# Second stage of a two-layer convolution: three tap products and a partial sum added by TensorE, moments on ScalarE

## Chip, cores and metric

The kernel runs on one core of a Trainium2 chip. The metric is the device time of one execution in microseconds (us); the time of the kernel before is the median of three runs.

## What is computed

The input x is (16, 512, 64, 64) in fp32. Two layers of the form x + conv(group_norm(x)) follow each other. The first is a 4x4 blur of every channel. The second, cut to what matters:

```python
x = x + _L0_conv_ref(_gn(x), L0_conv_kernel)
x = x + _L1_conv_ref(_gn(x), ...)

def _L1_conv_ref(x, w_v, w1, gn_gamma, gn_beta, w2, b2):
    t = relu(group_norm(d4_1x1(x, w1), gn_gamma, gn_beta, cmid))      # 256 channels
    wgt = einsum('oi,bighw->boghw', w2, t) + b2                       # 9 tap weights of each group and pixel
    ...                                                               # taps turned for each of 8 orientations
    pats = unfold_patches(d4_1x1(x, w_v), 3)                          # 3x3 patches of 512 channels
    return (wv * pats).sum(axis=4)                                    # sum of 9 products
```

So each output is a residual plus nine products of a tap weight with a shifted value.

## The kernel before

`stage_a` (the first quarter of the time) does the blur and is not touched. It leaves its result x1 in HBM. `stage_b` does the second layer, image by image.

**The pieces of an image.** On TensorE an image has eight chunks of 512 pixels a band: `forward` (L716, 4 PSUM banks a chunk), `block_v` (4 banks) and `block_t` (2 banks) by `block_of` (L726), and `inverse` (L742, 2 banks). They make the value maps `xm` and the map `t`. They are made during the period of the image before, at the steps that FORWARD_AT, BLOCK_V_AT, BLOCK_T_AT and INVERSE_AT name (L78 to L81). `values` (L749) turns `xm` into `val`, three granules ahead. `tap_weights` (L765) makes the nine tap weights of a quarter of the image (a unit) in PSUM banks 0 to 4.

**The granule.** An image has 16 granules of 4 channel maps (4 units by 4). For each, with 1024 elements a partition, VectorE (`granule`, L1127) makes six products of taps 3 to 8 (`pooled`, L1088) into the ring `prod_p` and, in two halves of 512 columns (`opening`, L1100), three products of taps 0 to 2 that it adds itself, with the residual, through PSUM bank 7 and into `acc`. GpSimd (L1018 to L1029) adds the six products of the ring, one after another, to `acc`. Each of its additions waits for its own last one by `p_added`. SP then stores `acc`, and had loaded the residual into it.

**The ring of banks.** All results that ScalarE fetches from PSUM (`forward`, `block`, `inverse`, `values`) go through the two banks 5 and 6. TensorE's `take` (L696) waits until ScalarE has emptied the bank two before, and ScalarE takes them in the same order.

**What sets the order.** Each engine has one queue written out by hand: a period of 16 steps, step n holding what belongs to granule n. TensorE's period is L825 to L844, ScalarE's L973 to L997, VectorE's L1157. At the end of a period `lead` (L790, L939) makes the first values and taps of the next image.

**The moments of t.** VectorE takes statistics of t (`t_stats`, `t_aggregate`), TensorE averages over partitions (`means`, `variances`), VectorE does the small arithmetic between (`t_spreads`, `t_add_eps`, `t_affine`, L1054 to L1074), GpSimd the power (`t_rstd_of`, L1012), ScalarE then `relu` (L932). The bias of a tap is added in PSUM by ScalarE (`tap_bias`, L925).

Of the kernel before, what the change touches and what calls it, by code (L numbers as in the profile page):

```python
# [24 lines left out]
ALU = mybir.AluOpType  # L25
# [42 lines left out]
D_TAPS, P_TAPS = (0, 1, 2), (3, 4, 5, 6, 7, 8)  # L68
NP = len(P_TAPS)
P_RING = 4  # L70
P_LATE = (4, 5)
HALF = 512
WV_BANKS = 5
ACC_RING = 4
# [7 lines left out]
LOAD_AT = {1: 1, 2: 2, 3: 3, 5: 4, 7: 5, 8: 6, 9: 7}  # L82
LOAD_NEXT_AT = 10
EDGES_AT = 13
RSTD_AT = (13, 5)
EDGES = 2
SETUP = 4
# [367 lines left out]
def stage_b(nc, ctx, sem, ps, x1, basis, wsrc, signs, w2t, w2mask, b2t, gamma, beta, mean_b, out, x1_scale, x1_bias):  # L455
    def sb(name, shape, dtype=F32):
# [7 lines left out]
    t_last = sb("t_last", [P, MT, BANDS * UPX])  # L464
# [12 lines left out]
    power = sb("power_b", [P, MT])  # L477
    six = sb("six_t", [P, MT, 2 * UNITS, 6])
# [12 lines left out]
    first_of = base[:, 3 * P:3 * P + 32]  # L491
    w_term = prod_p[:, 0, 0:2 * 4 * OQ * 16].rearrange("p (b c o) -> p b c o", b=2, c=4)
# [6 lines left out]
    sp_apart, act_apart, dve_apart = (sem(f"b_{e}_apart") for e in ("sp", "act", "dve"))  # L499
    setup = sem("b_setup")  # L500
# [11 lines left out]
    own = sem("own")  # L512
# [12 lines left out]
    OWN = 12  # L525
    EARLY, LATE = (0, 1, 2), (3, 4)
# [3 lines left out]
    def order_of_period(more):  # L530
        for n in range(N_GRAN):
            if n + AHEAD < N_GRAN:
                yield ("values", n + AHEAD), V_BANKS[n + AHEAD]
            if more:
                if n in BLOCK_V_AT:
                    yield ("block_v", BLOCK_V_AT[n]), QM
                for c in BLOCK_T_AT.get(n, ()):
                    yield ("block_t", c), MT
                if n in FORWARD_AT:
                    yield ("forward", FORWARD_AT[n]), IRR  # L540
                for c in INVERSE_AT.get(n, ()):
                    yield ("inverse", c), MT

    def order_at_first():
        yield ("forward", 0), IRR
        for c in range(CHUNKS):
# [4 lines left out]
            yield ("inverse", c), MT  # L551

# [13 lines left out]
    def taps_of(tap):  # L566
        return ps[:, tap // 2, tap % 2 * UPX:(tap % 2 + 1) * UPX]
# [16 lines left out]

    def t_end(i, u):

        return chunk_end(i, "inverse", 2 * u + 1)
# [5 lines left out]
    def bank_done(i, n, b):  # L593

        if b == 0:
            return own, i * (OWN * N_GRAN) + OWN * n + 8
        return p_done(i, n, P_TAPS.index(banks[b][-1]))

    def granule_done(i, n):

        return p_done(i, n, NP - 1)
# [26 lines left out]
    def _(sp):  # L628
# [11 lines left out]
        def load_resid(i, n):  # L640
# [29 lines left out]
        def period(i, more=True, ahead=True, begin=False):  # L670
            for n in range(N_GRAN):
# [19 lines left out]
    def _(pe):  # L691
# [11 lines left out]
        def affine():  # L703

            for kt in range(KT):
                q = slice(32 * kt, 32 * kt + 32)
                nc.tensor.matmul(ps[q, D_BANK, 0:B], first_of,
                                 x1_scale[:].rearrange("p (b k) -> p k b", k=KT)[:, kt, :], start=True, stop=True,
                                 skip_group_check=True)
                for r in range(IRR):  # L710
                    mm = nc.tensor.matmul(ps[q, D_BANK, (1 + r) * B:(2 + r) * B], forward_m[:, r, :],
# [53 lines left out]
        def tap_weights(i, u, which):  # L765
            pe.wait_ge(t_ready, i * (MT * UNITS) + MT * (u + 1))
            for b in which:
                if not first(i, u):
                    pe.wait_ge(*bank_done(i, GRANS * u - 1, b))
                for tap in banks[b]:  # L770
# [8 lines left out]

        def means(i):  # L780
            pe.wait_ge(t_local, i + 1)
            if not first(i):
                pe.wait_ge(*p_done(i, -3, NP - 1))
            nc.tensor.matmul(ps[:, STAT_BANK, MEAN0:MEAN0 + MT], blk[:], mv[:, :, 0], start=True, stop=True).then_inc(t_mean, 1)

        def variances(i):
            pe.wait_ge(t_spread, i + 1)
            nc.tensor.matmul(ps[:, STAT_BANK, VAR0:VAR0 + MT], blk[:], spread[:], start=True, stop=True)                .then_inc(t_var, 1)

        def lead(i):  # L790
# [34 lines left out]
        def period(i, more=True):  # L825
# [449 lines left out]
```

## Time and profile before

| | us |
|---|---|
| median of 3 runs | 5196.51 |
| fastest of them | 5195.63 |
| slowest of them | 7707.95 |
| the profiled execution's own time | 5195.25 |
| its span in the trace | 5193.5 |

The profiled execution has one core, so its span is that of all views. An engine is called busy while an instruction of it runs. Durations of neighbouring instructions of an engine overlap a little, so the pace of an engine is read from start to start. TensorE's clock is given as a share of 2.4 GHz; 0.50 is 1.2 GHz.

### The profile page before, as it was taken

The page shows a single profiled execution, that of the slowest core. Times are in us where ns is not written, and L with a number is a line of the kernel's source. Part 1 is how long each engine was busy: PE and PEld are TensorE (multiplying, and loading weights), DVE is VectorE, ACT ScalarE, POOL GpSimd, SP SyncE. Part 2 cuts the span into 40 slices and gives each one's busy share as a digit, 9 for nine tenths or more (in the row PEclk, how much of TensorE's full clock was granted, in tenths as well). Part 3 has the DMA queues.
Part 4 walks back from the last instruction along what each step waited for, and adds up shares of the span by engine and source line. Part 5 has one row for each costly group of instructions (what it writes and reads, how often), then busy time and mean ns, then how long its engine had stood idle before and what let it go on. Part 6 is the DMA issues. An engine that isn't in the chain of part 4 may idle for free.

```text
span 5193.5 us, 113938 instructions
## 1 busy us (share of the span) xinstructions
PE 3796.5 (73%) x36988; PEld 1315.4 (25%) x36988; DVE 4670.5 (90%) x8017; ACT 2854.0 (55%) x4642; POOL 4507.4 (87%) x2208
## 2 busy tenths in 40 slices
PE   8999999978766767676858685767676766767642
PEld 3333333322222222222222221222222222222220
DVE  6777777736999999999999999999999999999998
ACT  7999999956444535354545454444454444535421
POOL 5888888835999999999999999999999999999999
PEclk9999999989888888898889798989898988888866
DMA  7999999943333333232324242323232333333221
GB/s 235 257 257 257 257 256 256 247 107 100 105 102 102 99 106 107 92 121 83 119 83 130 83 127 85 120 91 115 91 110 91 110 103 102 99 106 107 82 74 57
DMA packets 872814, 679.40 MB, mean 131 GB/s; under 512 B 560080, under 2 KB 822736, under 8 KB 855888
## 3 DMA queue, kind: packets, MB, share of 16 engines
q1 hardware_dynamic: 872272, 672.72, 44.2%
q8 instruction: 273, 4.47, 0.4%
q14 instruction: 269, 2.20, 0.1%
HBM read 404.15 MB, written 268.44 MB: 130 GB/s over the span
## 4 chain that ended last, share of the span: by engine, by line
POOL 51%; DVE 13%; issue 9%; PE 4%; POOLq 1%; ACT 1%; DMA 0%; DVEq 0%; SPq 0%; ACTq 0%
POOL acc L1027 51%; DVE prod_p L1078 3%; DVE ps L1122 2%; DVE ps L1119 2%; DVE ps L1078 1%; DVE six_t L1043 1%; DVE acc L1125 1%; DVE prod_d L1078 1%; PE ps L722 1%; PE ps L732 1%; PE ps L773 1%; DVE dev_t L1059 1%; POOLq L1024 1%; DMA xr<-x 0%; POOLq L1026 0%
## 5 line engine op out<-in xcount | busy, mean ns | idle before, releaser
L1027 POOL TENSOR_TENSOR acc<-acc,prod_p 128x1024 f32<-128x1024 f32 x1536 | 3645.0, 2373 | 267.6 <-DVE acc L1125 50.4
L1078 DVE TENSOR_TENSOR prod_p<-ps,val 128x1024 f32<-128x1024 f32 x1536 | 1852.5, 1210 | 111.2 <-POOL acc L1027 110.7
L290 PE MATMUL ps<-xn,band 64*64 64x512 f32 x8192 | 949.2, 599 | 22.1 <-issue 13.7
L773 PE MATMUL ps<-t,w 128*32 128x256 f32 x9216 | 614.0, 425 | 435.7 <-ACT t L936 225.5
L760 PE MATMUL ps<-xm,base 128*32 128x256 f32 (+1 forms) x8192 | 636.2, 445 | 166.4 <-ACT val L923 73.7
L732 PE MATMUL ps<-xh,wh 128*32 128x512 f32 x6144 | 706.8, 600 | 49.6 <-ACT val L923 33.7
L1078 DVE TENSOR_TENSOR prod_d<-ps,val 128x512 f32<-128x512 f32 x1024 | 693.1, 677 | 25.7 <-ACT ps L929 24.0
L722 PE MATMUL ps<-xr,base 128*32 128x512 f32 x4096 | 547.1, 659 | 213.3 <-ACT val L923 124.1
L923 ACT ACTIVATE val<-ps 128x512 f32<-128x512 f32 (+1 forms) x640 | 339.8, 555 | 619.5 <-DVE prod_p L1078 418.0
L322 POOL TENSOR_TENSOR x_out<-x_out,x_in 128x512 f32<-128x512 f32 x512 | 636.2, 1275 | 0.0
L250 ACT ACTIVATE x_out<-ps 64x512 f32<-64x512 f32 x1024 | 606.1, 592 | 52.1 <-PE ps L290 31.8
L929 ACT ACTIVATE ps<-ps,b 128x256 f32<-128x256 f32 x576 | 235.2, 444 | 508.6 <-PE ps L773 506.8
L871 ACT ACTIVATE xh<-ps,xh_affine 128x512 f32<-128x512 f32 x512 | 395.1, 777 | 195.5 <-PE ps L722 180.0
L773 PEld LDWEIGHTS ps<-t,w 128*32 128x32 f32 x9216 | 309.2, 121 | 756.4 <-DVE ps L1119 219.6
L290 PEld LDWEIGHTS ps<-xn,band 64*64 64x64 f32 x8192 | 325.3, 132 | 434.0 <-issue 430.0
L337 POOL TENSOR_TENSOR rstd<-var_eps,power 128x8 f32 (+2 forms) x133 | 212.9, 1601 | 238.1 <-DVE var_eps L384 238.1
L879 ACT ACTIVATE xm<-ps 128x512 f32<-128x512 f32 x512 | 306.0, 598 | 190.4 <-PE ps L732 190.4
L760 PEld LDWEIGHTS ps<-xm,base 128*32 128x32 f32 x8192 | 251.2, 115 | 563.8 <-issue 186.4
L237 ACT ACTIVATE xn<-x_in,norm_b,rstd 128x512 f32<-128x512 f32 x512 | 389.5, 809 | 6.6
L916 ACT ACTIVATE val<-val 128x512 f32<-128x512 f32 x192 | 120.5, 628 | 436.7 <-DVE prod_p L1078 436.6
L1078 DVE TENSOR_TENSOR ps<-ps,val 128x512 f32<-128x512 f32 x512 | 351.2, 686 | 0.0
L1119 DVE TENSOR_TENSOR ps<-ps,acc 128x512 f32<-128x512 f32 x512 | 351.2, 686 | 0.0
(73 smaller groups left out, 3180.1 us busy)
## 6 DMA issues: line engine op xcount, KB each, us to landing
x_in<-x SPq DMA_DIRECT2D x128, 1024.0 KB, 7.4
x<-x_out SPq DMA_DIRECT2D x256, 512.0 KB, 5.2
xr<-x SPq DMA_DIRECT2D x512, 256.0 KB, 3.5
acc<-x SPq DMA_DIRECT2D x1024, 128.0 KB, 2.9
out<-acc SPq DMA_DIRECT2D x256, 512.0 KB, 2.7
prod_p<-wsrc SPq DMA_DIRECT2D x1, 384.0 KB, 4.6
w<-w2t SPq DMA_DIRECT2D x1, 288.0 KB, 4.6
shift_m<-shifts SPq DMA_DIRECT2D x1, 256.0 KB, 5.5
```

Source lines behind the costliest of these rows:

```text
L237: nc.scalar.activation(group(xn[:, r, :], XP, W, 2, g), group(x_in[:, k % X_RING, :], W, W, 0, g), ACT.Identity, bias=norm_b[:, k % 2, g:g ...
L250: nc.scalar.activation(group(x_out[H2 * t:H2 * t + H2, r, :], W, W, 0, 2 * two + x).rearrange("p m h w -> p m (h w)"), ps[at:at + H2, 2 * ...
L290: mm = nc.tensor.matmul(ps[to:to + H2, 2 * two + t, :], band[rows, v, rows], group(xn[rows, k % N_RING, :], XP, W, v, 2 * two + x), start= ...
L322: nc.gpsimd.tensor_tensor(out, out, group(x_in[:, k % X_RING, :], W, W, 0, g) .rearrange("p m h w -> p m (h w)"), ALU.add).then_inc(x_adde ...
L722: mm = nc.tensor.matmul(ps[32 * kt:32 * kt + 32, b, :], forward_m[:, r, :], xr[:, kt, :], start=True, stop=True, skip_group_check=True)
L732: mm = nc.tensor.matmul(ps[32 * r:32 * r + 32, b, :], wh[:, r, o, :], xh[:, c % 2, r, :], start=True, stop=True, skip_group_check=True)
L760: mm = nc.tensor.matmul(ps[32 * q:32 * q + 32, b, at:at + ROWS[u] * W], inverse_v[:, m + x, :], xm[:, q4, r0:r0 + ROWS[u] * W], start=True ...
L773: mm = nc.tensor.matmul(taps_of(tap)[32 * q:32 * q + 32, :], w2[:, kt, tap * 32:(tap + 1) * 32], t[:, kt, u, q * UPX:(q + 1) * UPX], start ...
L871: nc.scalar.activation(xh[:, c % 2, r, :], ps[:, b, :], ACT.Identity, bias=xh_affine[:, 1 + r, bass.ds(i, 1)], scale=xh_affine[:, 0, bass. ...
L1027: nc.gpsimd.tensor_tensor(acc[:, r, :], acc[:, r, :], prod_p[:, k % P_RING, :], ALU.add).then_inc(p_added, 1)
L1078: return nc.vector.tensor_tensor(dst.rearrange("p (m r w) -> p m r w", m=count, w=W), taps_of(tap).rearrange("p (m r w) -> p m r w", m=1, ...
L1119: nc.vector.tensor_tensor(ps[:, D_BANK, :], ps[:, D_BANK, :], acc[:, r, half], ALU.add).then_inc(own, 1)
```

## The change

In the text below sum 0 and sum 1 are the two calls of the new `sums` for a granule, and final 0 and final 1 those of the new `final`.

- GpSimd's partial sum is of taps 0 to 5. VectorE writes tap 0's product straight into a new tile `sum_p` (ring of 2), and GpSimd adds the products of taps 1 to 5 to it.
- VectorE writes the products of taps 6 to 8 in full width into `prod_d`.
- TensorE adds the four terms (three of `prod_d`, one of `sum_p`) by multiplying them with the identity in tiles of 64x64, in two halves of a granule. Each half is 4 terms by 4 matmuls of 256 columns.
- VectorE adds that sum and the residual into `acc`, 512 columns at a time (`final`). `acc` has a ring of 2 in place of 4. The order of the parts in `acc` is new, so the residual comes in 8 DMAs and not 4, and the host unpacks the output another way.
- The banks of the taps and of the ring are other ones (ring in banks 6 and 7; sums in the second halves of banks 4 and 5).
- The small arithmetic on the moments of t goes from VectorE to ScalarE (ten small activations and the two reads of PSUM). The tile `t_last` is gone.
- The steps at which the pieces are made are moved, and `lead` is dissolved into steps 15 and 0.

The diff, cut to its core:

```diff
-D_TAPS, P_TAPS = (0, 1, 2), (3, 4, 5, 6, 7, 8)
+P_TAPS, D_TAPS = (0, 1, 2, 3, 4, 5), (6, 7, 8)
+NA = NP - 1
-ACC_RING = 4
+S_RING = 2
+ACC_RING = 2
+TAP_BANKS = {0: (0, 1), 1: (2, 3), 4: (5,), 2: (4, 6), 3: (7, 8)}
-FORWARD_AT = {0: 0, 1: 1, 2: 2, 4: 3, 6: 4, 7: 5, 8: 6, 9: 7}
-BLOCK_V_AT = {1: 0, 2: 1, 4: 2, 5: 3, 8: 4, 9: 5, 12: 6, 13: 7}
-BLOCK_T_AT = {1: (0,), 2: (1,), 4: (2,), 5: (3,), 8: (4,), 9: (5,), 10: (6, 7)}
-INVERSE_AT = {1: (0,), 2: (1,), 4: (2,), 5: (3,), 8: (4,), 9: (5,), 11: (6, 7)}
+FORWARD_AT = {0: 0, 1: 1, 2: 2, 5: 3, 6: 4, 7: 5, 9: 6, 10: 7}
+INVERSE_AT = {2: (0,), 3: (1,), 5: (2,), 6: (3,), 9: (4,), 10: (5,), 13: (6, 7)}
+BLOCK_V_AT = {1: 0, 2: 1, 4: 2, 5: 3, 8: 4, 9: 5, 13: 6, 14: 7}
+BLOCK_T_AT = {1: (0,), 2: (1,), 4: (2,), 5: (3,), 8: (4,), 9: (5,), 12: (6, 7)}
+STATS_AT = {4: 0, 7: 1, 11: 2, 13: 3}
+MOMENTS_AT, EDGES_AT = 14, 14
+RSTD_AT = (14, 2)
...
 # SP, step n
-                if more or n + 2 < N_GRAN:
-                    load_resid(i, n + 2)
                 if not (begin and n == 0):
                     store(i, n - 1)
+                    if more or n + 1 < N_GRAN:
+                        load_resid(i, n + 1)
...
 # TensorE
+        def sums(i, n, half):
+            if half == 0:
+                wait_apart(pe, pe_apart, *d_done(i, n, ND - 1))
+                wait_apart(pe, pe_apart, p_added, i * (NA * N_GRAN) + NA * (n + 1))
+                if n % GRANS == GRANS - 1 and n < N_GRAN - 1:
+                    wait_apart(pe, pe_apart, tap_ready, tap_count(i, (n + 1) // GRANS, 4))
+            if not first(i, n + half):
+                wait_apart(pe, pe_apart, *(final_done(i, n, 0) if half else final_done(i, n - 1, 1)))
+            terms = [prod_d[:, j, :] for j in range(ND)] + [sum_p[:, n % S_RING, :]]
+            for j, term in enumerate(terms):
+                for t in range(2):
+                    for x in range(2):
+                        rows, to, at = slice(H2 * t, H2 * t + H2), H2 * (t ^ x), (2 * half + x) * UPX
+                        mm = nc.tensor.matmul(ps[to:to + H2, SUM_BANKS[1 - t], UPX:], same[rows, :],
+                                              term[rows, at:at + UPX], start=(j == 0), stop=(j == len(terms) - 1),
+                                              skip_group_check=True)
+            mm.then_inc(summed, 1)
...
+            for n in range(N_GRAN):
+                u = n // GRANS
+                if n % GRANS == 0:
+                    tap_weights(i, u, TAP_ORDER[2:4])
+                if more and n == MOMENTS_AT:
+                    means(i + 1)
+                if more and n in FORWARD_AT:
+                    forward(i + 1, FORWARD_AT[n])
+                if more:
+                    for c in INVERSE_AT.get(n, ()):
+                        inverse(i + 1, c)
+                if not (begin and n == 0):
+                    sums(i, n - 1, 0)
+                if more and n == MOMENTS_AT:
+                    variances(i + 1)
+                if n % GRANS == 0:
+                    tap_weights(i, u, TAP_ORDER[4:])
                 if n + AHEAD < N_GRAN:
                     values(n + AHEAD)
+                if more and n == N_GRAN - 1:
+                    pe.wait_ge(xm_edges, EDGES * (i + 2))
+                    values(0)
+                if not (begin and n == 0):
+                    sums(i, n - 1, 1)
                 if more:
                     if n in BLOCK_V_AT:
                         block_v(i + 1, BLOCK_V_AT[n])
                     for c in BLOCK_T_AT.get(n, ()):
                         block_t(i + 1, c)
...
                 if n % GRANS == GRANS - 1 and n < N_GRAN - 1:
-                    tap_weights(i, n // GRANS + 1, EARLY)
-            if more:
-                lead(i + 1)
+                    tap_weights(i, u + 1, TAP_ORDER[:2])
+                if more and n == N_GRAN - 1:
+                    values(1)
+                    tap_weights(i + 1, 0, TAP_ORDER[:1])
+                    values(2)
+                    tap_weights(i + 1, 0, TAP_ORDER[1:2])
...
 # GpSimd
-                for j in range(NP):
-                    nc.gpsimd.tensor_tensor(acc[:, r, :], acc[:, r, :], prod_p[:, k % P_RING, :], ALU.add).then_inc(p_added, 1)
+                for j in range(1, NP):
+                    nc.gpsimd.tensor_tensor(total, total, prod_p[:, k % P_RING, :], ALU.add).then_inc(p_added, 1)
...
 # VectorE, granule n
+            if not begin:
+                for j in range(ND):
+                    direct(i, n - 1, j)
...
+            pooled(i, n, 0)
+            pooled(i, n, 1)
             pooled(i, n, 2)
+            if not begin:
+                final(i, n - 1, 0)
             pooled(i, n, 3)
+            pooled(i, n, 4)
+            if not begin:
+                final(i, n - 1, 1)
+            pooled(i, n, 5)
```

ScalarE follows TensorE's order. Its step 15 is `t_affine`, `relu` of unit 0, `keep_values` 0, `keep_values` 1, bias of bank 0, `relu` 1, `keep_values` 2, bias of bank 1, `relu` 2.

## Rows read from the trace of the kernel before

**Rows 1.** The page: busy time of each engine, and the two costliest groups.

```profile
PE 3796.5 (73%) x36988; PEld 1315.4 (25%) x36988; DVE 4670.5 (90%) x8017; ACT 2854.0 (55%) x4642; POOL 4507.4 (87%) x2208
...
L1027 POOL TENSOR_TENSOR acc<-acc,prod_p 128x1024 f32<-128x1024 f32 x1536 | 3645.0, 2373 | 267.6 <-DVE acc L1125 50.4
L1078 DVE TENSOR_TENSOR prod_p<-ps,val 128x1024 f32<-128x1024 f32 x1536 | 1852.5, 1210 | 111.2 <-POOL acc L1027 110.7
```

**Rows 2.** Timeline of GpSimd, one period: start, duration (us), line, operation, idle before.

```profile
2189.91 0.71 POOL L1014 TENSOR_TENSOR rstd_t<-var_eps_t,power_b 128x2 f32<-128x2 f32 x1 [3.70 <-DVE var_eps_t L1065]
2190.59 14.82 POOL L1027 TENSOR_TENSOR acc<-acc,prod_p 128x1024 f32<-128x1024 f32 x6
2207.35 181.35 POOL L1027 TENSOR_TENSOR acc<-acc,prod_p 128x1024 f32<-128x1024 f32 x72 [1.94 <-DVE acc L1125]
...
2437.69 0.71 POOL L1014 TENSOR_TENSOR rstd_t<-var_eps_t,power_b 128x2 f32<-128x2 f32 x1 [3.71 <-DVE var_eps_t L1065]
```

**Rows 3.** Timeline of VectorE: the statistics of a unit; inside a granule.

```profile
1203.43 2.47 DVE L1043 BATCH_NORM_STATS2 six_t<-t_last 128x6 f32<-128x512 f32 x4 [17.32 <-ACT t_last L894]
...
1982.84 0.69 DVE L1119 TENSOR_TENSOR ps<-ps,acc 128x512 f32<-128x512 f32 x1
1983.43 1.21 DVE L1078 TENSOR_TENSOR prod_p<-ps,val 128x1024 f32<-128x1024 f32 x1
1984.56 0.69 DVE L1122 TENSOR_TENSOR ps<-ps,prod_d 128x512 f32<-128x512 f32 x1
```

**Rows 4.** Timeline of TensorE in its dense stretches of the second stage.

```profile
1995.31 1.93 PE L760 MATMUL ps<-xm,base 128*32 128x256 f32 x32
1997.29 5.49 PE L732 MATMUL ps<-xh,wh 128*32 128x512 f32 x48
2002.64 1.92 PE L722 MATMUL ps<-xr,base 128*32 128x512 f32 x16
2004.72 1.93 PE L722 MATMUL ps<-xr,base 128*32 128x512 f32 x16 [0.15 <-ACT xh L871]
2006.78 1.99 PE L747 MATMUL ps<-t,base 128*128 128x512 f32 x4
2008.70 1.93 PE L760 MATMUL ps<-xm,base 128*32 128x256 f32 x32
...
2139.01 5.39 PE L773 MATMUL ps<-t,w 128*32 128x256 f32 x96
```

**Rows 5.** Timeline of TensorE in the first stage, tiles of 64x64 and of 128x128 in turn.

```profile
602.75 3.70 PE L290 MATMUL ps<-xn,band 64*64 64x512 f32 x32
606.37 0.39 PE L271 MATMUL ps<-mv,ones 128*128 128x8 f32 x2
606.93 3.70 PE L290 MATMUL ps<-xn,band 64*64 64x512 f32 x32 [0.17 <-issue]
```

**Rows 6.** Instructions of ScalarE in one period by line and shape.

```profile
L929 ACT ACTIVATE ps<-ps,b 128x256 f32<-128x256 f32 x36 | 14.7, 443 | 33.0 <-PE ps L773 32.8
...
L936 ACT ACTIVATE t<-t,t_bias,t_scale 128x1024 f32<-128x1024 f32 x6 | 7.0, 1232 | 0.0
```

**Rows 7.** Timeline of TensorE: a `forward` after an idle stretch.

```profile
2072.76 6.60 PE L722 MATMUL ps<-xr,base 128*32 128x512 f32 x32 [6.48 <-ACT val L923]
```

**Rows 8.** Window of that stretch; last three columns: granted clock, DMA share, GB/s.

```profile
2072.00:2076.00 4.00, 3.24 (x16) 0.74 (x20) 4.00 (x7) 1.87 (x3) 3.71 (x3) 0.50 0.21 45
```

**Rows 9.** Timeline of GpSimd, last period: its second granule and its last.

```profile
4949.99 14.86 POOL L1027 TENSOR_TENSOR acc<-acc,prod_p 128x1024 f32<-128x1024 f32 x6 [0.17 <-DVE prod_p L1078]
...
5175.51 14.77 POOL L1027 TENSOR_TENSOR acc<-acc,prod_p 128x1024 f32<-128x1024 f32 x6 [0.17 <-POOL acc L1027]
```

**Rows 10.** Timeline of SP's queue: the four DMAs of a residual.

```profile
1984.28 1.85 SPq L650 DMA_DIRECT2D acc<-x  x4
```

**Rows 11.** The page, DMA issues: KB each, us from issue to landing.

```profile
acc<-x SPq DMA_DIRECT2D x1024, 128.0 KB, 2.9
out<-acc SPq DMA_DIRECT2D x256, 512.0 KB, 2.7
```

More of the change, by code:

```diff
@@ L566, in taps_of, with bank_of, tap_count @@
     def taps_of(tap):
-        return ps[:, tap // 2, tap % 2 * UPX:(tap % 2 + 1) * UPX]
+        bank = next(b for b in TAP_ORDER if tap in TAP_BANKS[b])
+        h = TAP_BANKS[bank].index(tap)
+        return ps[:, bank, h * UPX:(h + 1) * UPX]
+    def bank_of(tap):
+        return next(b for b in TAP_ORDER if tap in TAP_BANKS[b])
+    def tap_count(i, u, bank):
+        return i * (UNITS * len(TAP_ORDER)) + len(TAP_ORDER) * u + TAP_ORDER.index(bank) + 1
     def period_base(i):
@@ L591, in p_done, with d_done, bank_done, sums_done @@
         return p_ready, i * (NP * N_GRAN) + NP * n + j + 1
[L593 to L597, printed above, removed]
+    def d_done(i, n, j):
+        return d_ready, i * (ND * N_GRAN) + ND * n + j + 1
+    def bank_done(i, n, bank):
+        tap = TAP_BANKS[bank][-1]
+        return p_done(i, n, P_TAPS.index(tap)) if tap in P_TAPS else d_done(i, n, D_TAPS.index(tap))
+    def sums_done(i, n, half):
+        return summed, i * (2 * N_GRAN) + 2 * n + half + 1
+    def final_done(i, n, half):
+        return finished, i * (2 * N_GRAN) + 2 * n + half + 1
     def granule_done(i, n):
-        return p_done(i, n, NP - 1)
+        return d_done(i, n, ND - 1)
     def halo_count(i, n):
@@ L769, in tap_weights @@
                     pe.wait_ge(*bank_done(i, GRANS * u - 1, b))
-                for tap in banks[b]:
+                for tap in TAP_BANKS[b]:
                     for kt in range(MT):
@@ L849, in _ @@
         period(B - 1, more=False)
+        for half in range(2):
+            sums(B - 1, N_GRAN - 1, half)
     @block.scalar
@@ L882, in keep_block_t @@
         def keep_block_t(i, c):
-            if c >= CHUNKS - 2 and not first(i):
-                act.wait_ge(t_ready, i * (MT * UNITS))
             for m in range(MT):
@@ L962, in _ @@
             keep_inverse(0, c)
+        act.wait_ge(const_in, 16 * 6)
+        keep_means(0)
+        keep_variances(0)
         edges(0)
+        t_affine(0)
+        relu(0, 0)
         keep_values(0, 0)
-        relu(0, 0)
-        act.wait_ge(const_in, 16 * 6)
-        tap_bias(0, 0, EARLY + LATE)
+        tap_bias(0, 0, TAP_ORDER[:2])
         keep_values(0, 1)
@@ L994, in period @@
                 if n % GRANS == GRANS - 1 and n < N_GRAN - 1:
-                    tap_bias(i, u + 1, EARLY)
-            if more:
-                lead(i + 1)
+                    tap_bias(i, u + 1, TAP_ORDER[:2])
+                if more and n == N_GRAN - 1:
+                    keep_values(i + 1, 1)
+                    tap_bias(i + 1, 0, TAP_ORDER[:1])
+                    relu(i + 1, 1)
+                    keep_values(i + 1, 2)
+                    tap_bias(i + 1, 0, TAP_ORDER[1:2])
+                    relu(i + 1, 2)
         period(0)
@@ L1127, in granule, with final @@
+        def final(i, n, half):
+            r = n % ACC_RING
+            dve.wait_ge(*sums_done(i, n, half))
+            if half == 0:
+                dve.wait_ge(resid_in[r], i * (128 * N_GRAN // ACC_RING) + 128 * (n // ACC_RING + 1))
+            part = acc[:, r, half * HALF:(half + 1) * HALF].rearrange("p (s n) -> p s n", s=2)
+            total = ps[:, SUM_BANKS[0]:SUM_BANKS[1] + 1, UPX:]
+            nc.vector.tensor_tensor(part, total, part, ALU.add).then_inc(finished, 1)
         def granule(i, n, more, begin=False):
@@ L1194, in _ @@
         period(B - 1, more=False)
-        for j in P_LATE:
-            pooled(B - 1, N_GRAN - 1, j)
+        for j in range(ND):
+            direct(B - 1, N_GRAN - 1, j)
+        for half in range(2):
+            final(B - 1, N_GRAN - 1, half)
 PERMS = ((0, 1, 2, 3, 4, 5, 6, 7), (3, 0, 1, 2, 5, 6, 7, 4), (2, 3, 0, 1, 6, 7, 4, 5), (1, 2, 3, 0, 7, 4, 5, 6),
```

305 lines of the change are left out of this document (135 added, 170 removed).

## The prediction

> **What bounds the kernel now.** I read the page first. GpSimd and VectorE are the busy engines, TensorE is at 73% of the span, and the costliest group is GpSimd's additions into `acc`, of 2.37 us each [rows 1]. Then GpSimd's timeline, which shows how tight that chain is: 72 additions take 181.35 us without a pause, so 2.52 us from start to start, 0.15 of it the wait for its own last result. The power of the moments comes once an image and gives the period: 2437.69 - 2189.91 = 247.8 us [rows 2]. 96 additions by 2.52 are 241.9; the rest is the pause around the moments (3.70 waiting for the variance, 0.71 the power, 1.94 waiting for VectorE). So the second stage, three quarters of the time, runs at GpSimd's pace. The first stage isn't touched.
>
> **What the change does to each engine, by granule.** All paces are from start to start.
>
> GpSimd: 5 additions and not 6, of the same shape: 5 x 2.52 = 12.6 us, from 15.1 [rows 2].
>
> VectorE: a product of 1024 columns takes 1.13 us (1983.43 to 1984.56), an operation of 512 columns 0.60 [rows 3]. Nine products and two finals: 9 x 1.13 + 2 x 0.60 = 11.4 us. At steps 4, 7, 11 and 13 the statistics add 2.4 [rows 3]. The small arithmetic on the moments leaves it.
>
> TensorE: this is where the work goes. At full clock, in dense stretches: a chunk of `block` (6 banks) 5.35 us (1997.29 to 2002.64), so 3.57 for `block_v` and 1.78 for `block_t`; `forward` 4.14 (I use 4.1); `inverse` 1.92; `values` 1.95 for 32 instructions of 256 columns; 96 instructions for six taps 5.39, so 0.89 for a tap and 1.8 for a bank of two [rows 4]. For the four banks of 384 columns at an image's start I take 2.7, three quarters of 4 x 0.89. A half sum has 16 matmuls in tiles of 64x64. The first stage runs the same form with 512 columns, 32 instructions (two for each fp32 matmul, so 16 matmuls) in 602.75 to 606.37 = 3.62 us [rows 5]; with 256 columns that is 1.81. I take 1.8 for a half, 3.6 for a granule, 57.6 for an image. The image's other pieces: 8 `forward` 32.8, 8 `block` 42.8, 8 `inverse` 15.4, `values` 4 x 2.7 + 12 x 1.95 = 34.2, 36 taps 32. Together 215 us: below the old period, and above GpSimd's 16 x 12.6 = 202. TensorE becomes the fullest engine.
>
> But its work is lumpy, and the new order leaves little room to even that out. VectorE waits for sum 0 of granule n-1 at final 0, between its third and fourth product of granule n. GpSimd has by then only two products to add. So every step that is long on TensorE stops all three. I write P(n) for TensorE's time from the end of sum 0 of granule n-1 to that of granule n (`values` and bank 3 at unit starts, sum 1, `block`, taps, then `forward` and `inverse` of step n+1, sum 0): P(0) 12.2, P(1) 16.9, P(2) 12.8, P(3) 11.8, P(4) 18.7, P(5) 16.9, P(6) 9.7, P(7) 11.8, P(8) 18.7, P(9) 16.9, P(10) 5.6, P(11) 11.8, P(12) 14.8, P(13) 7.2, P(14) 7.2, P(15) 22.1. For instance P(4) = bank 3 1.8 + `values` 1.95 + sum 1 1.8 + `block` 5.35 + `forward` 4.1 + `inverse` 1.92 + sum 0 1.8.
>
> Two other limits stand against P(n). VectorE's cycle: 11.4, with statistics 13.8. And GpSimd's loop: from final 0 to the second product of the next granule is 10.3, five additions are 12.6, sum 0 with its wakeups 2.0: 24.9 for two granules, 12.5 for one. Going through the steps with all three, the distance from final 0 to final 0 is, for n from 1 to 15 and then 0: 16.9, 12.8, 12.1, 18.7, 16.9, 11.4, 13.8, 18.4, 16.9, 11.4, 13.8, 14.5, 14.4, 14.3, 22.1, 12.2. The sum is 240.6 us, against 247.8. So of the 40 us that GpSimd is spared in an image, TensorE's long steps take back all but 7.
>
> Now what a queue in order adds to that.
> - Step 15: ScalarE is behind. `relu` costs 1.2 an instruction, two for a unit, and a bias 0.44 [rows 6]. `relu` 1 stands ahead of `keep_values` 2, so `values(2)` finds its third bank not empty for about 2.6 us; `relu` 2 does the same to `forward(0)` for about 0.7. I take 3.3. `t_affine` and `relu` 0 come in the slack of step 14 and cost nothing; if the power of step 14 were late by more than 3 us, they would push into step 15 one for one.
> - Each half sum has waits of its own in TensorE's queue and changes the shape of the tiles and back. The first stage pays 606.93 - 606.37 = 0.56 for two such changes, two small instructions and a wait, 0.17 of it idle [rows 5]. So a half sum pays between 0 and 0.56; it counts only in the ten steps that TensorE sets. I take 0.15, near to that idle, as the small instructions are part of the 0.56: 20 x 0.15 = 3.0 (bounds 0 and 11.2).
> - The clock. After 6.48 us idle, a `forward` of four banks took 6.60 and not 4.1, at a clock of 0.50 [rows 7, 8]. The new order leaves TensorE idle for some 6 us in steps 10, 13 and 14. At 10 and 13 a slow sum is hidden, as GpSimd's next additions don't wait for it; ahead of step 15 it isn't: I take 2.0 (bounds 0 and 6).
>
> That makes 240.6 + 3.3 + 3.0 + 2.0 = 248.9 us a period, 1.1 more than now. Fifteen periods prepare a next image: +16.
>
> The last period has only `values`, taps and sums on TensorE, and goes at GpSimd's pace. Now it is 15.05 a granule, 241 for 16 [rows 9]; then 16 x 12.6 = 202, and behind it the last two sums and finals, 6. That saves 33, and less if the sums run at half clock (the loop is then 26.7 for two granules): I take 30, bounds 20 and 35.
>
> Costs that I set at nothing. The residual: the ring of 2 makes its load wait for the last store, but from final 1 it is 2.7 (landing of the store) + 8 issues at 0.46 + 2.9 = 9.3 us, and final 0 of that granule comes about 20 us later [rows 10, 11]. The loads of x1 stand in front of them in SP's queue, each waiting for a `forward` that TensorE has done by then. ScalarE's ten small activations replace VectorE's in step 14, in slack; without it they would cost some 2 us. The pause of 6.3 us around the moments [rows 2] goes.
>
> The sum: 5195 (own time of the profiled execution, 1.3 under the median) + 16 - 30 = 5181; to the median 5182.
>
> **Rivals.**
> - *The queue is smoother than I put it* (faster). Without relu stall, changes of tiles and cold clock: 240.6 a period, 15 x (-7.2) - 35 = -143, so 5053. For it: TensorE is at full clock wherever it is dense, and each P(n) is made of measured paces. If a long step could besides borrow from a short one by 1 us each, it would be 4900. Against: TensorE's queue is in order and the waits of sum 0 stand in it.
> - *Changing the tile shape costs TensorE at each half sum* (slower). It is one mechanism: 64x64 for the sums, 128x32 for all around. The row's ceiling is 0.56 a half sum [rows 5]; with it in the ten steps, 240.6 + 3.3 + 11.2 + 2.0 = 257.1, 15 x 9.3 - 25 = +115, so 5310. It turns the sign from 0.20 a half sum on, and costs over 2% from some 0.5. For it: nothing before switches in the second stage between 128x32 and 64x64. Against: in the first stage two switches, two instructions and a wait fit in that 0.56. The Trainium skill, TensorEngine Tiling, section Key Properties, says that changing the tiling mode (not just the tile) drains TensorE. By that rule 64 changes an image each empty the engine, and this rival is the one to expect; the first stage's row agrees that something is paid, and leaves open how much is the drain.
> - *The half sums are slower than half of a 512-column blur* (slower). A weight load of 64 columns for each 256 columns of moving data may not be hidden; the bound is the full 3.6 us of the 512-column row. At 2.6 a half: +16 a period, 5420. Against: taps with 256 columns run at 0.056 an instruction, half of 512's 0.111 [rows 4].
> - That the change doesn't do what it says I leave out: the operations are all there in the diff.
>
> **Chances.** Forecast (within 2%, about what a measurement tells from no change) 0.48. Smoother 0.27, faster by over 2% all of it. Tile changes 0.17 and slow half sums 0.08, slower by over 2%. The likeliest case's own range is 5100 to 5280. The range over the cases: 5030, where the smooth schedule and a little borrowing end, to 5330.
>
> **What would show it.** GpSimd's additions in groups of five at 2.52, with pauses of 4 to 7 us at steps 4, 5, 8, 9 and 15 released by VectorE, whose own idle time is at final 0 and released by the sums. TensorE over 80% busy in the second stage, at a clock above 0.9. Half sums of 1.8 to 1.95. Period 245 to 253 from power to power. The last period some 205. Wrong if VectorE's idle is at `tap_ready` or the residual, if half sums take over 2.2, or if the period is below 240.

## The result and the profile after

The changed kernel takes 5360.7 us (median of 4 runs, 5356.7 to 5362.7) against 5196.8. The ratio is 1.0315, with an interval of 1.0295 to 1.0335: 3% slower. I had forecast 5182, no change, with a range up to 5330, and it lies above that. The ratio and all comparisons below leave out two single runs that lie far off the rest, one of the kernel before (7708 us) and one of experiment 7 (10720 us).

The page of the kernel after: busy times, TensorE's clock in 40 slices, the chain that ended last, and the groups that answer to [rows 1].

```profile
PE 4678.5 (87%) x53372; PEld 1923.4 (36%) x53372; DVE 3950.6 (74%) x6113; ACT 2911.8 (54%) x4802; POOL 3903.2 (73%) x1953
...
PEclk9999999989999999999989898999999999999987
...
PE 52%; DVE 9%; issue 7%; POOL 6%; ACT 5%; DVEq 0%; POOLq 0%; ACTq 0%; DMA 0%; SPq 0%
...
L1128 POOL TENSOR_TENSOR sum_p<-sum_p,prod_p 128x1024 f32<-128x1024 f32 x1280 | 3041.4, 2376 | 1087.9 <-DVE prod_p L1154 1009.9
...
L833 PE MATMUL ps<-prod_d,base 64*64 64x256 f32 x12288 | 867.7, 417 | 426.4 <-POOL sum_p L1128 256.7
L1190 DVE TENSOR_TENSOR acc<-ps,acc 128x512 f32<-128x512 f32 x512 | 353.6, 691 | 923.9 <-PE ps L833 922.7
```

GpSimd got its 600 us less, and stands idle for 1088 us before its additions, waiting for products of VectorE. VectorE stands idle for 923 us before the finals (L1190), waiting for the sums of TensorE (L833). TensorE, 73% busy before, is now 87% busy and carries half of the chain. So the bound moved to TensorE, as I had put it; what that costs is where the forecast failed.

Timeline of GpSimd of the kernel after: the power of the moments in two neighbouring images, which answers to [rows 2].

```profile
2225.78 0.71 POOL L1116 TENSOR_TENSOR rstd_t<-var_eps_t,power_b 128x2 f32<-128x2 f32 x1
...
2485.22 0.72 POOL L1116 TENSOR_TENSOR rstd_t<-var_eps_t,power_b 128x2 f32<-128x2 f32 x1
```

This period is 259.4 us. I had forecast 248.9. The mean of 14 periods is 260.0, from 1450.17 to 5089.57; read the same way, the kernel before has 248.0. The 14 periods make 168 us of the 167 that the span grew. The first period adds 6.9, the start of the stage saves 2.5, and what stands behind the last power saves 4.8, where I expected 30 from the last period. So of the 179 us between forecast and result some 155 come from the periods and 25 from the end.

**Where in the period.** I go through it by the ends of sum 0 on TensorE, as the prediction did: step n is the time from the end of sum 0 of granule n-1 to that of granule n, so its last piece stands in step n+1 of the queue. The distances of one period in us:

| step | 1 | 2 | 3 | 4 | 5 | 6 | 7 | 8 | 9 | 10 | 11 | 12 | 13 | 14 | 15 | 0 |
|---|---|---|---|---|---|---|---|---|---|---|---|---|---|---|---|---|
| predicted | 16.9 | 12.8 | 12.1 | 18.7 | 16.9 | 11.4 | 13.8 | 18.4 | 16.9 | 11.4 | 13.8 | 14.5 | 14.4 | 14.3 | 22.1 | 12.2 |
| measured | 17.1 | 13.8 | 12.6 | 18.8 | 17.1 | 11.7 | 14.7 | 18.8 | 17.0 | 13.5 | 14.9 | 14.7 | 15.6 | 14.5 | 30.5 | 14.4 |

The period they make up is 259.4 us against 240.6. Of the 18.8 between them I had put 8.3 on top. Step 15 has 8.4 of it, steps 0 and 10 4.3, steps 7, 11 and 13 3.2, step 2 1.0.

Timeline of TensorE of the kernel after. First step 4, from the end of one sum 0 (2325.63) to that of the next (2344.40); then step 10; then step 15.

```profile
2325.63 1.93 PE L812 MATMUL ps<-t,w 128*32 128x256 f32 x32
2327.38 1.91 PE L799 MATMUL ps<-xm,base 128*32 128x256 f32 x32
2329.22 1.53 PE L833 MATMUL ps<-prod_d,base 64*64 64x256 f32 x24
2330.57 0.61 PE L833 MATMUL ps<-sum_p,base 64*64 64x256 f32 x8
2331.11 5.49 PE L771 MATMUL ps<-xh,wh 128*32 128x512 f32 x48
2336.46 1.93 PE L761 MATMUL ps<-xr,base 128*32 128x512 f32 x16
...
2340.60 1.98 PE L786 MATMUL ps<-t,base 128*128 128x512 f32 x4
2342.52 1.53 PE L833 MATMUL ps<-prod_d,base 64*64 64x256 f32 x24
2343.86 0.61 PE L833 MATMUL ps<-sum_p,base 64*64 64x256 f32 x8
2344.40 1.93 PE L799 MATMUL ps<-xm,base 128*32 128x256 f32 x32
...
2433.46 2.84 PE L833 MATMUL ps<-prod_d,base 64*64 64x256 f32 x24 [6.01 <-POOL sum_p L1128]
2436.04 1.10 PE L833 MATMUL ps<-sum_p,base 64*64 64x256 f32 x8
2437.08 2.55 PE L799 MATMUL ps<-xm,base 128*32 128x256 f32 x32
...
2506.12 1.47 PE L799 MATMUL ps<-xm,base 128*32 128x384 f32 x16
2509.90 2.69 PE L799 MATMUL ps<-xm,base 128*32 128x384 f32 x16 [2.31 <-ACT val L1018]
2512.35 2.47 PE L812 MATMUL ps<-t,w 128*32 128x256 f32 x32
2517.31 4.25 PE L812 MATMUL ps<-t,w 128*32 128x256 f32 x48 [2.49 <-DVE prod_p L1154]
```

Step 4 is dense, and each piece has the price of [rows 4]. A half sum takes 1.89 (2329.22 to 2331.11) where I had 1.8 + 0.15, so the changes of tile shape cost no more than I had put. In step 10 TensorE is idle for 6.01 us and the half sum then takes 3.6 (2433.46 to 2437.08). Step 15 shows three losses: 2.3 for ScalarE's `relu` 1, a gap of 2.5 that I had not seen coming, and slow matmuls behind each gap (rows of 2.69 for 1.47, 2.47 for 1.91, 4.25 for some 2.7; from start to start some 3 us in all).

Windows of the half sum in step 10 and behind the two gaps of step 15; the last three columns are clock, DMA share, GB/s.

```profile
2433.00:2437.00 4.00, 3.54 (x32) 1.97 (x32) 3.12 (x3) 0.39 (x1) 1.85 (x1) 0.50 0.37 108
2510.00:2512.00 2.00, 2.00 (x16) 0.71 (x20) 0.88 (x1) 0.72 (x2) 0.95 (x1) 0.51 0.25 72
2518.00:2520.00 2.00, 2.00 (x24) 0.95 (x20) 0.00 (x0) 0.45 (x1) 1.57 (x1) 0.50 0.01 4
```

The clock is 0.50 in the first and the third and 0.51 in the second, so 1.2 GHz.

### The profile page after: what moved, and what is told of

Same layout as the page of the kernel before. It is cut to its first block, busy times and chain, and to the rows that moved or that the text cites. A ratio compares the mean times of both kernels' runs of the same rounds, so it can differ in the third digit from the quotient of the medians.

```text
span 5360.9 us, 147175 instructions
## 1 busy us (share of the span) xinstructions
PE 4678.5 (87%) x53372; PEld 1923.4 (36%) x53372; DVE 3950.6 (74%) x6113; ACT 2911.8 (54%) x4802; POOL 3903.2 (73%) x1953
## 4 chain that ended last, share of the span: by engine, by line
PE 52%; DVE 9%; issue 7%; POOL 6%; ACT 5%; DVEq 0%; POOLq 0%; ACTq 0%; DMA 0%; SPq 0%
PE ps L833 17%; PE ps L771 11%; PE ps L799 8%; PE ps L812 7%; POOL sum_p L1128 6%; PE ps L786 5%; PE ps L761 4%; DVE prod_p L1154 4%; DVE prod_d L1154 3%; ACT xh L936 3%; DVE six_t L1143 2%; ACT t L1029 1%; ACT ps L1024 1%; DVE acc L1190 0%; ACT val L1018 0%
## 5 line engine op out<-in xcount | busy, mean ns | idle before, releaser
L1128 POOL TENSOR_TENSOR sum_p<-sum_p,prod_p 128x1024 f32<-128x1024 f32 x1280 | 3041.4, 2376 | 1087.9 <-DVE prod_p L1154 1009.9
L1154 DVE TENSOR_TENSOR prod_p<-ps,val 128x1024 f32<-128x1024 f32 x1280 | 1514.6, 1217 | 86.0 <-ACT ps L1024 86.0
L833 PE MATMUL ps<-prod_d,base 64*64 64x256 f32 x12288 | 867.7, 417 | 426.4 <-POOL sum_p L1128 256.7
L1190 DVE TENSOR_TENSOR acc<-ps,acc 128x512 f32<-128x512 f32 x512 | 353.6, 691 | 923.9 <-PE ps L833 922.7
L293 PE MATMUL ps<-xn,band 64*64 64x512 f32 x8192 | 948.0, 598 | 22.9 <-issue 15.5
L1154 DVE TENSOR_TENSOR prod_d<-ps,val 128x1024 f32<-128x1024 f32 x768 | 889.5, 1215 | 20.2 <-issue 17.2
L833 PEld LDWEIGHTS ps<-prod_d,base 64*64 64x64 f32 x12288 | 475.3, 143 | 839.3 <-issue 729.1
L799 PE MATMUL ps<-xm,base 128*32 128x256 f32 (+1 forms) x8192 | 596.1, 429 | 39.8 <-ACT val L1018 37.0
L812 PE MATMUL ps<-t,w 128*32 128x256 f32 x9216 | 562.0, 394 | 62.2 <-DVE prod_d L1154 29.8
L761 PE MATMUL ps<-xr,base 128*32 128x512 f32 x4096 | 495.0, 601 | 25.7 <-ACT xh L936 11.6
L812 PEld LDWEIGHTS ps<-t,w 128*32 128x32 f32 x9216 | 295.1, 114 | 327.3 <-issue 93.4
```

What stands on the lines that cost most here:

```text
L293: mm = nc.tensor.matmul(ps[to:to + H2, 2 * two + t, :], band[rows, v, rows], group(xn[rows, k % N_RING, :], XP, W, v, 2 * two + x), start= ...
L761: mm = nc.tensor.matmul(ps[32 * kt:32 * kt + 32, b, :], forward_m[:, r, :], xr[:, kt, :], start=True, stop=True, skip_group_check=True)
L799: mm = nc.tensor.matmul(ps[32 * q:32 * q + 32, b, at:at + ROWS[u] * W], inverse_v[:, m + x, :], xm[:, q4, r0:r0 + ROWS[u] * W], start=True ...
L812: mm = nc.tensor.matmul(taps_of(tap)[32 * q:32 * q + 32, :], w2[:, kt, tap * 32:(tap + 1) * 32], t[:, kt, u, q * UPX:(q + 1) * UPX], start ...
L833: mm = nc.tensor.matmul(ps[to:to + H2, SUM_BANKS[1 - t], UPX:], same[rows, :], term[rows, at:at + UPX], start=(j == 0), stop=(j == len(ter ...
L1128: nc.gpsimd.tensor_tensor(total, total, prod_p[:, k % P_RING, :], ALU.add).then_inc(p_added, 1)
```

## Experiments

All start from the changed kernel, except where the text names another. Times are medians; "change" is its 5361.

**1. One term of four** (leaves the products of taps 6 to 8 out of the output).

```diff
-            terms = [prod_d[:, j, :] for j in range(ND)] + [sum_p[:, n % S_RING, :]]
+            terms = [sum_p[:, n % S_RING, :]]
```

> The sums on TensorE take only the partial sum of GpSimd (one term of four); the products of taps 6 to 8 are still made by VectorE but left out of the output. Theory A (TensorE's queue sets the pace of the long steps): a half sum falls from 1.89 us to 0.54, TensorE's work by 43 us an image, the period from 259.4 to 222 to 230 us, the time to 4810 to 4930. Theory B (the time is in the chain of waits between the engines, not in the length of TensorE's work): the period falls by under 15 us, the time stays above 5130.

Measured: 4946 us (two runs), 415 less; the distance between two powers fell to about 234. That is A, 16 us over its range. Some 42 us an image were taken from TensorE (32 half sums, of 0.59 in place of 1.89 from start to start) and about 26 came back. Steps 5, 8 and 9 fell by 2.6 each, which is two half sums in full: there the length of TensorE's work sets the pace. In TensorE's timeline a half sum is now short, and the waits are VectorE's:

```profile
2413.71 0.66 PE L833 MATMUL ps<-sum_p,base 64*64 64x256 f32 x8 [1.88 <-DVE prod_d L1154]
2414.30 1.93 PE L799 MATMUL ps<-xm,base 128*32 128x256 f32 x32
2417.31 0.66 PE L833 MATMUL ps<-sum_p,base 64*64 64x256 f32 x8 [1.07 <-DVE acc L1190]
```

**2. A loop over two images.**

```diff
-        with pe.Fori(1, B - 1) as i:
-            period(i)
+        with pe.Fori(0, (B - 2) // 2) as i2:
+            period(i2 * 2 + 1)
+            period(i2 * 2 + 2)
```

and so on the other engines.

> Each engine's loop runs 7 times over two images in place of 14 times over one; nothing else. Theory L (going back to the loop's start costs TensorE 2.5 us in the middle of the long step 15, and some more through the clock behind it): 7 boundaries less, the time falls by 18 to 28 us, to 5333 to 5343; in the trace every second period has no gap of 2.5 us ahead of the taps of banks 4 and 2. Rival M (that gap is a wait for VectorE's product): no change, 5361 within 5.

Measured: 5338 us, 23 less, in the middle of theory L. Step 15 takes 26.7 us inside an iteration and still 30.5 at its start. TensorE's timeline of this version, step 15 in two neighbouring periods:

```profile
2247.32 2.68 PE L801 MATMUL ps<-xm,base 128*32 128x384 f32 x16 [2.30 <-ACT val L1021]
2249.76 5.07 PE L814 MATMUL ps<-t,w 128*32 128x256 f32 x80
...
2503.20 2.56 PE L801 MATMUL ps<-xm,base 128*32 128x384 f32 x16 [2.31 <-ACT val L1021]
2505.51 2.60 PE L814 MATMUL ps<-t,w 128*32 128x256 f32 x32
2510.57 4.33 PE L814 MATMUL ps<-t,w 128*32 128x256 f32 x48 [2.45 <-DVE prod_p L1159]
```

Inside an iteration the 80 instructions of five taps run through. At the loop's start the gap of 2.45 stands between 32 and 48, with a product of VectorE named as its releaser. The same work inside an iteration has no gap, so the gap comes with the loop's start and isn't that product.

**3. The same on the kernel before.**

> The kernel before with its loops over two images instead of one, nothing else. Theory L2 (the way back to the loop's start costs TensorE the same 2.5 to 3 us there, but it lies in TensorE's slack behind GpSimd): no change, 5192 within 8. Rival (the loop's start costs time in any kernel of this kind): 15 to 30 us less.

Measured: 5201 against 5194, ratio 1.0014 (1.0005 to 1.0024): 7 us longer, 1 us over the range of L2, and no gain. TensorE's timeline of the kernel before has the gap too, in slack:

```profile
2219.21 5.10 PE L760 MATMUL ps<-xm,base 128*32 128x384 f32 x32 [3.08 <-issue]
```

So the loop's start is hidden in the kernel before, where TensorE waits for others anyway, and it is a cost of this change to have put it on the path.

**4. relu late.** `relu` of units 1, 2, 3 from steps 15 and 0 to steps 0, 2 and 6.

```diff
-                    relu(i + 1, 1)
                     keep_values(i + 1, 2)
                     tap_bias(i + 1, 0, TAP_ORDER[1:2])
-                    relu(i + 1, 2)
...
+                if n in (0, 2, 6):
+                    relu(i, {0: 1, 2: 2, 6: 3}[n])
```

> relu of units 1, 2 and 3 goes from step 15 and step 0 to steps 0, 2 and 6, behind that step's keep_values. Theory S (relu 1 holds up values(2) for 2.3 us in step 15, and the idle TensorE then falls to half clock): the period falls by 2.3 to 4.5 us, the time to 5290 to 5325. Rival (step 15 is set by the tap bank that VectorE waits for, or by the loop's start): 5350 or more.

Measured: 5313 us, 47 less, 3.1 a period. Theory S. TensorE's timeline in step 15:

```profile
2494.50 3.02 PE L799 MATMUL ps<-xm,base 128*32 128x384 f32 x32
2497.34 1.91 PE L812 MATMUL ps<-t,w 128*32 128x256 f32 x32
2502.83 5.35 PE L812 MATMUL ps<-t,w 128*32 128x256 f32 x48 [3.59 <-issue]
```

`values(2)` runs through in 3.02. The gap at the loop's start is now 3.59 and named "issue", and the taps behind it take 5.35 for 2.7. One loss covers part of another.

**5. Other steps for the next image's pieces.**

```diff
-FORWARD_AT = {0: 0, 1: 1, 2: 2, 5: 3, 6: 4, 7: 5, 9: 6, 10: 7}
-INVERSE_AT = {2: (0,), 3: (1,), 5: (2,), 6: (3,), 9: (4,), 10: (5,), 13: (6, 7)}
-STATS_AT = {4: 0, 7: 1, 11: 2, 13: 3}
+FORWARD_AT = {1: 0, 2: 1, 5: 2, 6: 3, 9: 4, 10: 5, 11: 6, 12: 7}
+INVERSE_AT = {3: (0,), 4: (1,), 7: (2,), 8: (3,), 11: (4,), 12: (5,), 13: (6, 7)}
+STATS_AT = {4: 0, 8: 1, 12: 2, 13: 3}
```

with `block` at 1, 2, 5, 6, 9, 10 and the loads to match.

> Only the tables of steps change: forward at steps 1, 2, 5, 6, 9, 10, 11, 12; inverse at 3, 4, 7, 8, 11, 12, 13; block at 1, 2, 5, 6, 9, 10 and 12 to 14; the loads of x1 and the statistics with them. TensorE's longest steps in the middle fall from 18.7 and 16.9 us to about 15, and the short ones fill; the work is the same. Theory C (lumps: VectorE and GpSimd stop in every long step and can't catch up in the short ones): the period falls by 12 to 20 us, the time to 5060 to 5180. Theory D (TensorE's total and its waits count, not how it is spread): no change, above 5300.

Measured: 5293 us, 68 less, 4 us a period. It fits neither: C was three to four times too big. By the steps (means of 14 periods), 1 to 9 give back 7.8 us, steps 10 and 11 take 6.4 and steps 12 and 13 1.6 more. The spreading alone gained nothing; what remains is step 15, down from 29.9 to 25.8 since `forward` 0 has left it. The trace shows two reasons. The first is that steps 10 and 11 are now long ones of 17.0 and 17.8 us, with TensorE dense. Its timeline in step 11:

```profile
2421.32 6.25 PE L812 MATMUL ps<-t,w 128*32 128x256 f32 x112
...
2431.51 1.98 PE L786 MATMUL ps<-t,base 128*128 128x512 f32 x4
```

The second is in step 4, which takes 17.5 where some 15 was expected. Timeline of TensorE, then of VectorE:

```profile
2311.80 1.53 PE L833 MATMUL ps<-prod_d,base 64*64 64x256 f32 x24
2313.14 0.61 PE L833 MATMUL ps<-sum_p,base 64*64 64x256 f32 x8
...
2322.04 2.84 PE L833 MATMUL ps<-prod_d,base 64*64 64x256 f32 x24 [4.36 <-DVE prod_d L1154]
```
```profile
2313.82 0.69 DVE L1190 TENSOR_TENSOR acc<-ps,acc 128x512 f32<-128x512 f32 x1 [2.52 <-PE ps L833]
2314.43 1.22 DVE L1154 TENSOR_TENSOR prod_p<-ps,val 128x1024 f32<-128x1024 f32 x1
2315.56 2.46 DVE L1143 BATCH_NORM_STATS2 six_t<-t 128x6 f32<-128x512 f32 x4
2317.94 3.47 DVE L1154 TENSOR_TENSOR prod_d<-ps,val 128x1024 f32<-128x1024 f32 x3
```

Sum 1 ends at 2313.75; final 1, a product, the statistics and three products follow; sum 0 can start at 2322, and runs at half pace. VectorE waits for both halves of a sum. My schedule let only final 0 wait.

**6. TensorE kept busy.** Dummy matmuls, whose results nobody uses, ahead of the sums 0 that follow an idle stretch.

```diff
+            for _ in range(count):
+                nc.tensor.matmul(ps[0:32, SUM_BANKS[1], UPX:], blk[:, 0:32], w2[:, 0, 0:UPX], start=True, stop=True,
+                                 skip_group_check=True)
```

> Single dummy matmuls of 256 columns are put in TensorE's queue ahead of sum 0 where it idles 4 to 7 us: 12 in step 11 (ahead of sum 0 of granule 10), 8 in step 14, 9 in step 15, and 12 in the steps of the last period that begin no unit. They write where sum 0 will write, and are overwritten. Theory H (a sum 0 at half clock takes 3.9 us and not 1.9, and this is on the path at steps 10, 13 and 14 and in the last period): 5 to 7 us a period and 15 to 25 in the last, the time 5235 to 5290. Rival (as predicted: hidden at 10 and 13): 5300 to 5330. If the dummies themselves delay the sums: above 5350.

Measured: 5281 us, 80 less. Theory H. The mean clock of the run is 0.985, from 0.951. In step 11 of the queue (granule 10's sum 0), the dummies fill the idle time, and the sum is at full pace:

```profile
2415.54 5.34 PE L824 MATMUL ps<-w,blk 128*32 128x256 f32 x24 [0.91 <-DVE acc L1200]
2420.81 1.53 PE L841 MATMUL ps<-prod_d,base 64*64 64x256 f32 x24
2422.15 0.61 PE L841 MATMUL ps<-sum_p,base 64*64 64x256 f32 x8
```

By the steps, 13 fell by 1.7 us, 10 by 1.5 and 15 by 1.0. What stands behind the last power fell by 8 us, not by 15 to 25. Why so little was not tested; in some of these steps sum 0 still waits 0.6 to 2.7 us for GpSimd behind the dummies.

The Trainium skill, TensorE: Matmul & The Clock Gate (section Part 1: The HAM clock gate), has the idle clock at half rate and activity releasing it. These rows agree: 0.50 after 6 us idle, and 1.9 in place of 3.6 us for the half sum when TensorE had been busy.

**7. Statistics early**: between VectorE's third product and final 0.

```diff
             pooled(i, n, 2)
+            if more and n in STATS_AT:
+                t_stats(i + 1, STATS_AT[n])
...
             if not begin:
                 final(i, n - 1, 0)
```

> VectorE takes the statistics of t (2.4 us) between its third product and final 0, where it waits for sum 0, and not behind the sixth, ahead of the three products that sum 0 of this granule needs. Theory V (at steps 7, 11 and 13 the chain sum 1, final 1, sixth product, statistics, three products, sum 0 sets the step): these steps fall from 14.7, 14.9 and 15.6 us to 12.6 to 13.5, the period by 4 to 6 us, the time to 5270 to 5300. Rival W (sum 0 waits there for the bias of the tap banks by ScalarE): no change, 5350 to 5365.

Measured: 5329 us (three runs), 32 less. The way is V's, and the size some 40% of it. As means of 14 periods, step 11 fell from 15.0 to 13.3, step 13 from 15.6 to 14.9, and step 7 stayed at 14.6. In step 7 it varies from 13.3 to 15.5; in a period with 15.5 the statistics delay final 0, and with it sum 1:

```profile
2369.34 2.37 PE L833 MATMUL ps<-prod_d,base 64*64 64x256 f32 x24 [2.00 <-DVE acc L1190]
```

**8 and 9. The mends together**: 2, 4 and 7 (three), and with 5 (four).

> The same without the spread tables: loop of two images, relu late, statistics early, at the change's own steps. If they add up: 5361 - 23 - 47 - 75 = 5216, within 25. If step 15 has one cost counted twice in the loop and the relu: 20 more.

Measured: 5249 us, 33 above the sum that was expected. The three alone gave 23 + 47 + 32 = 102 less; together 112.

> Loop of two images, relu late, statistics early and the spread tables together. If the four are separate costs and the statistics were what held the spread version at its steps 4 and 8 (17.4 us there, with sum 0 at half clock): 5361 - 23 - 47 - 75 - 68 - 60 to 100 = 5050 to 5110, below the kernel before. If the spread steps are held by something else: 5140 to 5180.

Measured: 5078 us, ratio to the kernel before 0.9775 (0.9759 to 0.9792). Spread tables gave 68 alone and 171 on top of the three. That is what one expects of limits that cover each other: with the statistics out of the round, the steps 4 and 8 that had taken 17.5 and 17.3 take 13.9 and 13.4. Steps 10 and 11 stay at 17.0 and 17.7, the longest but step 15.

**10. Four mends and dummies** in step 15 and in the last period.

> The version with four mends (5078 us) and dummy matmuls ahead of sum 0 in step 15 (10) and in the steps of the last period that begin no unit (12). Theory H: the sum 0 of granule 14 falls from 3.9 to 1.9 us and what follows it isn't slow either, 2 to 3 us a period and 20 in the last: 5010 to 5030. Rival (the slack ahead of step 15 hides it): 5050 to 5060, from the last period alone.

Measured: 5042 us, 35 less, between the two. The period fell by 2.3 us, as H has it, and the time behind the last power by 9 and not by 20.

**11. Four mends and sum 1 early**: in the first step of a unit, sum 1 stands ahead of the values.

```diff
+                if n % GRANS == 0 and not (begin and n == 0):
+                    sums(i, n - 1, 1)
                 if n + AHEAD < N_GRAN:
                     values(n + AHEAD)
...
-                if not (begin and n == 0):
+                if n % GRANS != 0:
                     sums(i, n - 1, 1)
```

> The version with four mends, and in the first step of each unit TensorE does sum 1 ahead of the values and not behind them. Theory R (the round of final 0, sum 1, final 1, sixth product, three products, sum 0 passes twice between VectorE and TensorE and is a limit of its own, 13 us or more where bank 3 and the values stand ahead of sum 1): the waits of 1.8 to 2.0 us of sum 0 in steps 1, 5 and 9 go, 5 to 6 us a period, 4985 to 5010. Rival (these waits are VectorE's own cycle, with or without sum 1): 5070 or more.

Measured: 5029 us, 48 less, between R and its rival: 3.3 us a period and not 5 to 6. The wait for VectorE's products goes, as R has it, but part of it comes back from another side. Sum 0's wait, first in step 8 of the version with four mends, then in step 4 of this one:

```profile
2312.08 1.53 PE L835 MATMUL ps<-prod_d,base 64*64 64x256 f32 x24 [1.99 <-DVE prod_d L1155]
```
```profile
2482.59 1.53 PE L835 MATMUL ps<-prod_d,base 64*64 64x256 f32 x24 [1.15 <-POOL sum_p L1130]
```

Now GpSimd's last addition is late. Step 8 fell from 13.4 to 12.8.

**12. All of it.**

> Four mends, dummy matmuls and sum 1 early together. If both add up: 4915 to 4955. If TensorE's own work (218 us an image) begins to set the period, less is left of it: 4960 to 4990.

Measured: 4990 us, ratio to the kernel before 0.9610 (0.9594 to 0.9626), 371 below the change. The dummies and sum 1 early gave 35 and 48 alone and 88 together, so they did add up. It is above the first range, since each alone had given less than expected, and just at the upper end of the second; that TensorE's own work takes something from the sum is therefore not shown. TensorE's window over two periods of it shows 94% busy at a clock of 0.99, where the change had 87% and 0.95:

```profile
2139.00:2611.00 472.00, 443.97 (x5608) 185.75 (x5601) 388.24 (x387) 238.88 (x408) 381.63 (x163) 0.99 0.33 109
```
```profile
2226.00:2746.00 520.00, 451.82 (x5588) 187.03 (x5584) 390.36 (x390) 239.78 (x409) 382.66 (x164) 0.95 0.30 99
```

## Why the prediction was wrong

**What held.** GpSimd's additions (2.45 to 2.52 from start to start within a group), VectorE's products and finals, each of TensorE's pieces: all at their predicted prices. TensorE is the fullest engine (226 us busy a period), and the long steps 1, 4, 5, 8, 9 came within 0.4 us. That the others stop in them is what experiment 1 shows, where steps 5, 8 and 9 shrink by all that TensorE is spared, and experiment 9, where shorter steps 4 and 8 shorten the period; experiment 5 by itself doesn't show it. The residual cost nothing: VectorE's waits of any size are for TensorE and ScalarE, none for a DMA.

**The rival of the tile changes fell.** I gave it 0.17 and up to 0.56 us a half sum. The half sum takes 1.89, which is 0.08 over half of the 512-column row [rows 5]. Experiment 1 gives a second measure: 24 instructions fewer take 1.30 less, so 0.054 each, and the 8 that are left take 0.59, which is 0.16 more than 8 of these. So two changes of shape cost 0.08 to 0.16 us, near to the 0.15 that I took and far from the 0.56. Slow half sums fell too, by the 1.89. The rule of the Trainium skill, TensorEngine Tiling (Array Packing), section Key Properties, that a change of mode drains TensorE may hold, but its price here is at most that 0.16, changes in and out included. The result came out on the slower side by a mechanism that no rival named.

**The steps that failed.** I had 248.9 us a period and it is 259.4, and 30 us from the last period of which 4.8 came. By what they cost a period:
- *Step 15* (predicted 22.1 + 3.3, measured 30.5). The stall behind `relu` 1 was named and was 2.3 us. Missing was the loop's start, 2.5 us: it had been in the trace before as idle time in slack, and this change dissolved `lead`, so that tap banks, `forward` and sum 0, for all of which others wait, come right behind it. Missing too was that the matmuls behind each gap are slow, some 3 us in this step. Experiments 2 and 4.
- *The half clock* (I took 2.0). "At 10 and 13 a slow sum is hidden, as GpSimd's next additions don't wait for it." They do: VectorE stands at final 0, and the fourth to sixth product of the granule come behind it, so the additions of these wait. Experiment 6 got back 80 us, some 5 a period, where my account had 2; steps 10 and 13 gave 1.5 and 1.7 of it.
- *The two other limits.* I drew the round between VectorE and TensorE through final 0 alone. It goes through sum 1, final 1, the sixth product, statistics, three products and sum 0 as well. That is 14.4 us at step 0 (predicted 12.2), and it adds to step 11. Experiments 5, 7, 11. At steps 7 and 11 the round has one leg more: VectorE's last products free a bank, TensorE makes taps in it, ScalarE adds their bias, and only then does sum 0 start. Step 7 of the change, where two waits of TensorE show it:

```profile
2382.39 1.93 PE L812 MATMUL ps<-t,w 128*32 128x256 f32 x32 [0.99 <-DVE prod_d L1154]
2385.92 1.53 PE L833 MATMUL ps<-prod_d,base 64*64 64x256 f32 x24 [1.59 <-ACT ps L1024]
```

  No run took this leg alone. That rounds were left out is the step of the prediction that was wrong in its logic, not in a size.
- *Step 2*: `inverse` directly behind its own `block_t` waits 0.8 us for ScalarE to empty the bank. This is read from the trace; no run tested it.
- *The last period* (30 predicted, 4.8 measured): TensorE waits some 6 us in most granules there, so 13 of its 16 sums 0 are slow, 3.6 us, in a round of about 13.9 us a granule, where I had 12.6. My text had the loop at 26.7 for two granules as a bound, 13.35 for one, and then took a value near to the other end. Even the bound was too low.

These account for the 18.8 us over the bare schedule but for some 2, which are 0.1 to 0.5 in each of the other steps.

What stays open: why the loop's start costs TensorE 2.5 to 3.6 us (only that it goes when there is none is shown); why so little came back in the last period; and the parts of the change that no run took alone, the moments on ScalarE and the ring of 2.

**The bare idea isn't what lost.** The same arithmetic, with only the order in the queues changed and loops over two images, is at 5078, and with dummies and sum 1 early at 4990.

## What to carry to other kernels

When work goes to an engine that has slack on average, add up what its in-order queue holds between two points at which the others wait for it, step by step: the longest steps set the time, and short steps give nothing back. Draw every round between two engines through all of its waits, and count again what used to lie in the slack of the engine that gets fuller: loop starts, stalls behind another's copy, and the slow clock after idle time. In the rows shown here, waits of TensorE of 2.3 to 6 us cost their length and then 1.4 to 2.7 us more in the matmuls behind them. And a step that is made shorter by moving work makes another one longer: add that one up too.

## What the runs showed of the hardware that I had not expected

- The start of a loop's iteration holds TensorE's queue for 2.5 to 3.6 us, and the matmuls behind it are slow. In the version with four mends, the stretch from the end of sum 1 in step 15 to the end of the next sum 0 takes 18.9 us with a loop's start in it and 13.7 without.
- 29 dummy matmuls an image, which compute nothing (and 12 in most steps of the last one), made a kernel 80 us faster (1.5%); the mean clock of TensorE rose from 0.951 to 0.985.
- 64 changes of tile shape an image between 64x64 and 128x32 or 128x128 cost 0.08 to 0.16 us for each half sum, two changes.
